# Attention and expert kernel on one core: prologue on VectorE, V projected ahead of q and k, values in four matmuls with a last sum on GpSimd

## What is computed

```python
def bi_wkv(r, k, v, w, u, time_emb):        # forward and backward decayed sums over T
    tf = sigmoid(sum(time_emb, -1))[:, None, None]
    decay = exp(-exp(w))[None, :] * (0.5 + 0.5 * tf[:, :, 0])
    ek = exp(minimum(k, 30.0)); ekv = ek * v
    nf, df = scan(ekv), scan(ek); nb, db = reverse scans
    euk = exp(minimum(u + k, 30.0))
    base = sigmoid(r) * ((nf + nb - ekv + euk * v) / maximum(df + db - ek + euk, 1e-8))
    return base * (0.8 + 0.2 * tf)
def attn(x, W_K, W_Q, W_V, W_O):            # 16 heads of 128, causal
    k, q, v = (einsum('ihd,bpd->biph', W, x) for W in (W_K, W_Q, W_V))
    z = softmax(masked(q k^T) / sqrt(128)) v
    return einsum('df,bqf->bqd', W_O, z_flat)
def ffn(x, gate_w, expert_w, expert_b):     # 8 experts, top 2, softmax of the two gates
    ...
x = x + attn(bi_wkv(x, fside, fside, w, u, cond), ...)
x = x + ffn(bi_wkv(x, fside, fside, w2, u2, cond), ...)
```

## Time and profile before

| | us |
|---|---|
| median of 3 runs | 388.52 (388.48 to 388.64) |
| the profiled execution, its own time | 388.69 |
| its span (first to last instruction) | 386.8 |
| TensorE busy | 357.1 (92%), 2534 matmuls |
| VectorE busy | 315.2 (81%) |
| ScalarE busy | 219.7 (57%) |
| GpSimd busy | 210.1 (54%) |

### The profile page before, as it was taken

One profiled execution on the slowest core, in us unless ns is written; L12 is line 12 of the kernel. 1 busy time (PEld: TensorE's weight loads), 2 busy tenths in 40 slices (PEclk: granted clock), 3 DMA queues, 4 the chain that ended last, 5 costly groups with the idle time before them and its releaser, 6 DMA issues.

```text
span 386.8 us, 7608 instructions
## 1 busy us (share of the span) xinstructions
PE 357.1 (92%) x2534; PEld 332.8 (86%) x2534; DVE 315.2 (81%) x883; ACT 219.7 (57%) x616; POOL 210.1 (54%) x231
## 2 busy tenths in 40 slices
PE   0578888999999999999999999999999998999996
PEld 0467878999999899999999999999999987877885
DVE  3979988897889788988988898889757694676675
ACT  3648567648655766775667576665666463221000
POOL 3677977645553567956865776677554333110000
PEclk9999899999999999999999999999999999999999
DMA  6651050010000000031100004100000000000000
GB/s 219 217 170 50 0 164 2 19 39 1 2 0 2 1 3 2 11 110 47 53 3 2 1 20 146 56 2 1 3 0 2 2 1 3 0 14 14 28 29 27
DMA packets 4598, 14.14 MB, mean 37 GB/s; under 512 B 840, under 2 KB 1872, under 8 KB 3920
## 3 DMA queue, kind: packets, MB, share of 16 engines
q1 hardware_dynamic: 4416, 13.65, 10.6%
q10 hardware_dynamic: 144, 0.00, 0.0%
HBM read 12.60 MB, written 1.05 MB: 35 GB/s over the span
## 4 chain that ended last, share of the span: by engine, by line
PE 81%; DVE 10%; issue 2%; POOL 2%; ACT 2%; DMA 1%; SPq 0%; DVEq 0%; ACTq 0%; POOLq 0%
PE psQK L850 9%; PE psQK L852 9%; PE psQK L851 9%; PE psT L910 5%; PE psZ L850 4%; PE psO L852 4%; PE psO L850 4%; PE psO L851 4%; PE psS L901 4%; PE psS L850 4%; PE psZ L852 4%; PE psZ L851 4%; PE psS L851 4%; PE psS L852 4%; PE psV L850 4%; PE psV L852 3%
## 5 line engine op out<-in xcount | busy, mean ns | idle before, releaser
L472 ACT ACTIVATE prob<-prob,ntop 128x256 f32<-128x256 f32 (+1 forms) x128 | 57.3, 449 | 93.3 <-DVE ntop L690 93.3
L301 POOL TENSOR_SCALAR prob<-prob,rsum 128x128 f32<-128x128 f32 x64 | 38.9, 607 | 104.7 <-DVE rsum L698 104.7
L850 PE MATMUL psQK<-y_hi,w_hi 128*128 128x256 f32 x256 | 73.3, 286 | 1.3 <-DVE y_lo L613 1.1
L852 PE MATMUL psQK<-y_hi,w_lo 128*128 128x256 f32 x256 | 73.0, 285 | 0.0
L851 PE MATMUL psQK<-y_lo,w_hi 128*128 128x256 f32 x256 | 72.9, 285 | 0.0
L302 POOL TENSOR_SCALAR prob<-prob,rsum 128x256 f32<-128x256 f32 x64 | 59.8, 935 | 0.0
L266 POOL TENSOR_TENSOR w_lo<-raw,w_hi 128x512 fp32r<-128x512 f32 x40 | 52.9, 1334 | 6.6 <-ACT w_hi L356 6.4
L850 PEld LDWEIGHTS psQK<-y_hi,w_hi 128*128 128x128 f32 x256 | 49.3, 193 | 2.2 <-DVE y_lo L613 1.3
L852 PEld LDWEIGHTS psQK<-y_hi,w_lo 128*128 128x128 f32 x256 | 49.3, 193 | 0.0
L851 PEld LDWEIGHTS psQK<-y_lo,w_hi 128*128 128x128 f32 x256 | 49.3, 193 | 0.0
L702 DVE TENSOR_TENSOR qk<-psQK,qk 128x512 fp32r<-128x512 f32 x64 | 43.6, 682 | 6.5 <-ACT qk L460 4.8
(11 more groups left out here) (176 smaller groups left out, 1044.3 us busy)
## 6 DMA issues: line engine op xcount, KB each, us to landing
raw<-in_weights SPq DMA_DIRECT2D x5, 1024.0 KB, 6.5
raw<-in_weights SPq DMA_DIRECT2D x10, 512.0 KB, 4.2
out<-fT SPq DMA_DIRECT2D x8, 128.0 KB, 2.0
fT<-in_fT SPq DMA_DIRECT2D x2, 256.0 KB, 6.5
xT<-in_xT SPq DMA_DIRECT2D x2, 256.0 KB, 8.4
fT<-in_fT SPq DMA_DIRECT2D x1, 512.0 KB, 10.2
xT<-in_xT SPq DMA_DIRECT2D x1, 512.0 KB, 10.9
wu<-in_wu ACTq DMA_DIRECT2D x1, 4.0 KB, 1.6
```

What stands on the lines that cost most here:

```text
L301: pool.tensor_scalar(prob[:, k, 0:P], prob[:, k, 0:P], rsum[:, k, 0:1], None, ALU.mult)
L472: ins = act.activation(prob[:, k, lo:hi], prob[:, k, lo:hi], ACT.Exp, scale=-1.0, bias=ntop[:, k, q:q + 1], accum_out=ssum[:, k, q:q + 1])
L850: pe.matmul(out, ah, bh, start=first and k == 0, stop=False)
L852: ins = pe.matmul(out, al, bh, start=False, stop=last and k == n - 1)
```

## The change

1. *values*: the transposed probabilities pT are stored without their zero block, high and low side by side (3 x 128 columns each). Four matmuls take the place of six: v_hi of key block 0 against high and low of both query blocks (512 columns, the whole bank psZ), v_lo against the high part (256), and for key block 1 v_hi and v_lo against high and low of the second query block (2 x 128 columns each). So the low part's products are summed in the second half of psZ. z_high copies both halves (512 columns, z_two), z_low subtracts as before, and a new GpSimd addition, z_last, adds the second half to z_lo; output waits for it. z_last(u - 3) stands at the head of unit u on GpSimd, ahead of its list and of shares(u).
2. *V order*: project_v stands right behind scores(u), V(0, 0) ahead of scores(0). v_high stands behind exps(u), v_low behind reciprocals(u).
3. *Prologue*: SP loads f0 first and waits for it before the next load; temb goes to ScalarE's queue. The three products of GpSimd are gone: f_ekv and f_eukv are made on VectorE in PSUM; ScalarE saves one exp and its double copies of euk. WARM is 5.
4. *Places*: min and exps of a cond stand a unit earlier; refills of V units stand in "M" for groups above 1; shares of units 2 and 3 run on ScalarE; the tile y2 is gone, y2 lives in the cond tiles.
5. *End*: gates_copy(0) stands in unit 62, gates_turn(1) behind the output in unit 63, pT_high(63) ahead of tanh(2), y2_last(3) ahead of gate_last(2), and `late` is shifted by one in three places.

```diff
-DVE_PLACES = {"min": (-2, "E"), "xd": (0, "M"), ...
+DVE_PLACES = {"min": (-3, "E"), "xd": (0, "M"), ...
-ACT_PLACES = {"exps": (-1, "E"), "sxd": (0, "E"), ...
+ACT_PLACES = {"exps": (-2, "E"), "sxd": (0, "E"), ...
+SHARES_ACT = (2, 3)
-WARM = 7
+WARM = 5
-    pT = sb("pT", [P, 2, 2, 4 * P], F32R)
-    z_hi = sb("z_hi", [P, 2, GH, T], F32R)
+    pT = sb("pT", [P, 2, 2, 3 * P], F32R)
+    z_two = sb("z_two", [P, 2, GH, 2, T], F32R)
+    z_hi = z_two[:, :, :, 0]
-    f_ek, f_euk = halves(psQK[0]), halves(psS[0])
+    f_ek, f_ekv, f_euk, f_eukv = (halves(bank) for bank in (psQK[0], psQK[1], psS[0], psT))
 sync:
-        sp.dma_start(temb[:], ap["temb"]).then_inc(in_temb, 16)
         load_f(0, 1, in_f0)
+        sp.wait_ge(in_f0, 16)
         load_qk(0)
 gpsimd:
-        pool.memset(pT[:, :, :, 0:P].bitcast(F32), 0.0).then_inc(consts, 1)
+        def z_last(u):
+            i, h = u // GH, u % GH
+            pool.wait_ge(z_half, u + 1)
+            pool.tensor_tensor(z_lo[:, i % 2, h], z_lo[:, i % 2, h].bitcast(F32), z_two[:, i % 2, h, 1].bitcast(F32),
+                               ALU.add).then_inc(z_ready, 1)
-        pool.tensor_tensor(t0[:, EKV], t0[:, EK], cols(fT, 0), ALU.mult).then_inc(f_pool, 1)
-        pool.tensor_scalar(t0[:, EUK], t0[:, EUK], EXP_LIMIT, None, ALU.min).then_inc(f_pool, 1)
-        pool.tensor_tensor(f_eukv, t0[:, EUK], cols(fT, 0), ALU.mult).then_inc(f_pool, 1)
         for u in range(UNITS):
+            if u >= 3:
+                z_last(u - 3)
             for f, args in work.get(u, ()):
                 f(*args)
-            shares(u)
+            if u not in SHARES_ACT:
+                shares(u)
+        for u in range(UNITS - 3, UNITS):
+            z_last(u)
 scalar:
-            act.activation(z_hi[:, i % 2, h], psZ[:, 0:T], ACT.Copy).then_inc(z_hi_done, 1)
+            act.activation(z_two[:, i % 2, h], halves(psZ), ACT.Copy).then_inc(z_hi_done, 1)
-                at(u, "E", refill, kind, g, part)
+                at(u, "M" if u % GH < TT and g > 1 else "E", refill, kind, g, part)
         for u in range(UNITS):
             exps(u)
+            if h < TT and u:
+                v_high(i, h)
             do(u, "M")
...
+            if u in SHARES_ACT:
+                shares(u)
...
-            if h < TT:
-                v_high(i, h)
 vector:
+        dve.tensor_tensor(f_ekv, f_ek, cols(fT, 0), ALU.mult).then_inc(f_dve, 1)
...
+        dve.scalar_tensor_tensor(f_eukv, f_euk, EXP_LIMIT, cols(fT, 0), ALU.min, ALU.mult).then_inc(f_dve, 1)
...
         for u in range(UNITS):
-            if 1 <= u:
-                i, h = (u - 1) // GH, (u - 1) % GH
-                if h < TT:
-                    v_low(i, h)
             maxima(u)
             do(u, "M")
             reciprocals(u)
+            i, h = u // GH, u % GH
+            if h < TT:
+                v_low(i, h)
 tensor, values(u):
-            three(psZ[:, 0:T],
-                  [(both(v_hi, v_lo, ALL, i % 2, kb, slice(h * DH, (h + 1) * DH)),
-                    (pT[:, k, 0, (1 - kb) * T:(2 - kb) * T], pT[:, k, 1, (1 - kb) * T:(2 - kb) * T]))
-                   for kb in range(TT)]).then_inc(pv_done, 1)
+            heads = slice(h * DH, (h + 1) * DH)
+            second = psZ[:].rearrange("p (a n) -> p a n", a=2)[:, :, P:T]
+            pe.matmul(psZ[:], v_hi[:, i % 2, 0, heads], pT[:, k, :, P:3 * P], start=True, stop=False)
+            pe.matmul(psZ[:, 0:T], v_lo[:, i % 2, 0, heads], pT[:, k, 0, P:3 * P], start=False, stop=False)
+            pe.matmul(second, v_hi[:, i % 2, 1, heads], pT[:, k, :, 0:P], start=False, stop=False)
+            pe.matmul(second, v_lo[:, i % 2, 1, heads], pT[:, k, :, 0:P], start=False, stop=True).then_inc(pv_done, 1)
 tensor, units:
+        project_v(0, 0)
             scores(u)
+            if h < TT and u:
+                project_v(i, h)
...
-            if h < TT:
-                project_v(i, h)
-            elif i:
+            if h >= TT and i:
                 output(i - 1, h - TT)
-        late = {7: [(logits, 3)], 9: [(gates_turn, 2)], 10: [(base, 2)], 11: [(gates_turn, 3)], 12: [(base, 3)]}
+        late = {8: [(logits, 3)], 9: [(gates_turn, 2)], 10: [(base, 2)], 12: [(gates_turn, 3)], 13: [(base, 3)]}
```

More of the change, by code:

```diff
@@ L178, in cols @@
         return t[:, b]
+    y2 = [tiles[:, b % 2, GD + b // 2] for b in range(B)]
     def halves(bank):
         return bank[:].rearrange("p (c n) -> p c n", c=2)
-    f_ek, f_euk = halves(psQK[0]), halves(psS[0])
+    f_ek, f_ekv, f_euk, f_eukv = (halves(bank) for bank in (psQK[0], psQK[1], psS[0], psT))
     f_xd, f_xn = [psV[:, 0:T], psS[1][:, 0:T]], [psZ[:, 0:T], psO[:, 0:T]]
     t0 = tiles[:, 0]
-    f_e1, f_eukv = t0[:, XD], t0[:, XN]
+    f_e1 = t0[:, XD]
     def w_view(t, kind, part):
@@ L310, in y2_low @@
             pool.wait_ge(y2hi_done, b + 1)
[L311 removed]
+            pool.tensor_tensor(cols(y_lo, b), y2[b], cols(y_hi, b).bitcast(F32), ALU.subtract).then_inc(y2lo_done, 1)
         work = {}
@@ L379, in _ @@
         for c in range(CB):
-            act.activation(f_euk[:, c], fT[:, 0, c], ACT.Exp, bias=wu[:, 1, c:c + 1]).then_inc(f_act, 1)
-        for c in range(CB):
-            act.wait_ge(f_dve, 4 + c)
+            act.wait_ge(f_dve, 5 + c)
             scaled(f_xn[c], 0, c, 0).then_inc(f_act, 1)
@@ L474, in exps, with shares @@
             ins.then_inc(exped, 1)
+        def shares(u):
+            k = u % 2
+            act.wait_ge(recipd, u + 1)
+            act.activation(prob[:, k, 0:P], prob[:, k, 0:P], ACT.Copy, scale=rsum[:, k, 0:1])
+            act.activation(prob[:, k, P:3 * P], prob[:, k, P:3 * P], ACT.Copy, scale=rsum[:, k, 1:2]).then_inc(shared, 1)
         def pT_high(u):
@@ L507, in _ @@
         at(62, "E", gate_exp, 1)
-        at(63, "M", gates_copy, 0)
+        at(62, "E", gates_copy, 0)
         at(63, "E", gates_copy, 1)
@@ L522, in _ @@
         qk_high(1)
+        v_high(0, 0)
         cond(1)["exps"]()
         for u in range(UNITS):
+            i, h = u // GH, u % GH
             exps(u)
+            if h < TT and u:
+                v_high(i, h)
             do(u, "M")
@@ L533, in _ @@
             do(u, "E")
-            i, h = u // GH, u % GH
-            if h < TT:
-                v_high(i, h)
         z_high(UNITS - 2)
+        pT_high(UNITS - 1)
         tanh(2)
-        pT_high(UNITS - 1)
         z_high(UNITS - 1)
@@ L834, in _ @@
         add_experts(5)
+        y2_last(3)
         gate_last(2)
-        y2_last(3)
         add_experts(6)
         add_experts(7)
+        add_experts(8)
         gate_first(3)
-        add_experts(8)
+        add_experts(9)
         gate_last(3)
-        for j in range(9, 8 * B):
+        for j in range(10, 8 * B):
             add_experts(j)
@@ L949, in logits @@
                 for c in range(CB):
-                    ins = pe.matmul(bank[:, o:o + E], y2[:, b, c, t * P:(t + 1) * P], gate_w[:, c], start=c == 0, stop=c == CB - 1)
+                    ins = pe.matmul(bank[:, o:o + E], y2[b][:, c, t * P:(t + 1) * P], gate_w[:, c], start=c == 0, stop=c == CB - 1)
             ins.then_inc(logits_done, 1)
@@ L1006, in _ @@
         pe.matmul(ts, ones[:], temb[:], start=True, stop=True).then_inc(tsummed, 1)
-        pe.wait_ge(consts, 3 + E)
-        pe.wait_ge(f_dve, 6)
+        pe.wait_ge(consts, 2 + E)
+        pe.wait_ge(f_dve, 7)
         for n in range(WARM):
             for c in range(CB):
-                pe.matmul(psQK[1][:, c * T:(c + 1) * T], identf[:], fT[:, 0, c], start=True, stop=True)
+                pe.matmul(psQK[0][:, c * T:(c + 1) * T], identf[:], fT[:, 0, c], start=True, stop=True)
         pe.wait_ge(wlo_qk, 2)
-        pe.wait_ge(f_dve, 18)
+        pe.wait_ge(f_dve, 20)
         project_qk_half(0, 0)
@@ L1043, in _ @@
             if u == UNITS - 1:
+                gates_turn(1)
                 base(0)
```

80 lines of the change are left out of this document (37 added, 43 removed).

## The result

The changed kernel takes **386.71 us** (median of 20 runs, 383.48 to 388.60) against 388.52 before (388.30 to 388.69): a ratio of 0.9954, 95% interval 0.9938 to 0.9970. It is faster by 1.8 us, where 16.2 were forecast (372.3), and outside the forecast's range of 368 to 380. The runs of before lie within 0.4 us, those of after spread over 5, longer where the mean granted clock was lower (383.48 at 0.994, 387.7 to 388.6 at 0.978), and the profiled execution is among the long ones (388.28, span 386.5, clock 0.981). So stages are compared between profiles, and kernels by their medians.

The account below looks back on a forecast made before the run. TensorE was taken to bound the kernel from 63.4 us on, VectorE from 27.0 to 63.4. Gains 6.8 + 3.1 - 2.0 + 4.0 + 1.5 + 2.8 = 16.2 gave 372.3 us, range 368 to 380.

Parts of the forecast that it names:

- z_last, priced at nothing: GpSimd's 64 additions, at most 0.67 us each, fit its free time and cost nothing if the cover holds.
- rival (e): Steady units: z_last holds VectorE and pushes GpSimd's products onto scans; 5.1 us a unit, 408 us in all; 6%.
- the half microsecond spare takes it: Steady units: VectorE's spare time per unit absorbs a hold by z_last of at most 0.67 us.
- Values, 6.8: Units 7 to 59: four matmuls for six save 0.1275 us of TensorE a unit, 6.8 us gained.
- rival (c): Values: the new matmul forms cost the old time, so 7.3 us is missing, 379.6 us; 5%.
- V order, 3.1: Values in one unit of eight: TensorE's 0.62 us wait for V's low part goes, five times, 3.1 us gained.
- pT's new waits, -2.0: Units with V: pT's copies have less time before values; 0.15 us a block, 2.0 us lost.
- Rival (a): Units with V: pT becomes late in every block, 0.65 us in each of 14, 379.4 us; 15%.
- Start, 4.0: Before scores(0): f0 lands earlier and additions read PSUM, so q/k's second half starts 4.35 us earlier; 4.0 us gained.
- rival (b): Start: f0 no faster alone, or idle time lowers the clock; 1.5 of 5.5 us stay, 376.3 us; 12%.
- First seven units, 1.5: VectorE-bound first units: a TensorE wait at 60.87 can go and shares move to ScalarE; 1.5 us gained.
- End, 2.8: After 301.5 us: single TensorE waits go through moved pieces, less z_last(63)'s delay and disturbance; 2.8 us gained.

Follow-up runs that it names:

- no_sum: Changed kernel without the 64 GpSimd additions z_last, the second half of the bank copied but never added: 377.64 us.
- undo_values: Changed kernel with values back to six matmuls into half the bank and no GpSimd addition; prologue and V order stay new: 382.75 us.
- vorder_alone: Kernel before with only the new order of V, and the refills and cond pieces moved with it: 387.21 us.
- prologue_alone: Kernel before with only the new prologue and tail, y2 tiles and shares of units 2 and 3 on ScalarE: 384.91 us.

## Why the prediction failed, point by point

Cut at the starts of scores of units 0, 7 and 63, the profiled executions of before, of after and of the kernel without the addition are:

| stretch | before | after | no_sum | gain forecast | gain of after |
|---|---|---|---|---|---|
| to scores(0) | 27.04 | 26.07 | 24.40 | 4.0 | 1.0 |
| to scores(7) | 36.40 | 38.34 | 37.96 | 1.5 | -1.9 |
| to scores(63) | 257.89 | 258.25 | 249.45 | 7.9 | -0.4 |
| to the end | 65.5 | 63.8 | 63.8 | 2.8 | 1.7 |

The addition accounts for 9.1 us of the miss. Without it the kernel (377.64) lands inside the range, still 5.3 above the 372.3; these lie in the start, the first units and the end.

- **z_last, priced at nothing: the step that failed.** The prediction added nothing to the sum for it beyond a share of the 2.0 of new waits. It cost 8.8 us between scores(7) and scores(63) (258.25 for 249.45), and 9.1 by the medians. Of the 8.8, 7.0 had come by scores(55); the last 1.8 lie where the clock stood at half from 318 to 321 us in the changed kernel and not in no_sum. Its own duration was sized well enough (0.75 us for the estimated 0.67), and both effects had been named, in rival (e): that it holds VectorE and that it pushes the other products onto the scans. The error was "the half microsecond spare takes it". VectorE's added busy time is (35.46 - 32.80) / 8 = 0.33 us a unit, below that half microsecond and far below the 0.74 from which (e) was said to decide. But it doesn't come evenly. It comes in units with scans, 1.5 us at once, and the low part of V that TensorE waits for stands right behind: 0.85 us of TensorE in one unit, nothing in the next. A spare that is a mean over eight units was set against a load that falls on a few. Rival (e) had the right mechanism at too high a price, a unit of 5.1 us where 4.5 came in this period (36.04 / 8) and 4.6 on the mean of units 7 to 62, so the result lies between the forecast's range and (e), where no case of mine stood.
- **Values, 6.8: the matmuls as forecast, somewhat less of it in the time.** From 194.73 to the turn at 195.31 the four matmuls take 0.58 us, for 0.59 forecast, so rival (c) is out; a period falls by 1.00 us between undo_values and no_sum, 0.125 a unit. From scores(7) to scores(55), 48 units, it is 4.9 us (216.14 less 211.21) for the 6.1 that 0.1275 a unit gives; the earlier periods gained less. By the medians of these two it is 5.1 us.
- **V order, 3.1: right between the profiles.** From scores(7) to scores(55) vorder_alone takes 216.08 us for 219.22, 3.1 less with pT's new waits included; by the medians it is 1.4. It also laid three pairs of scans beside GpSimd's products, which the forecast had not.
- **pT's new waits, -2.0: in few places, not in every block.** In the periods of no_sum and undo_values shown above TensorE never waits. In no_sum three waits ahead of psZ stand between scores(7) and scores(63), 0.50, 0.54 and 1.36 us. The 7.5 us ahead of psZ in the changed kernel are five waits: 3.0 and 1.3 in the first units, 1.6 near the end and only two of 0.78 in between, in 14 blocks. Rival (a) is out.
- **Start, 4.0: 1.0 came, for two reasons.** f0 landed at 3.95 (3.6 forecast; its lower bound was the time of 128 KB on the way out, and f0 is 256 KB on the way in), but temb, 1 KB, now first in ScalarE's queue, landed at 4.10, and the chain runs from it. The first scan began at 6.04 for 7.58 before, 1.5 us earlier and not 2.6. That temb's own path would be the longer one I had not weighed:

```profile
0.73 3.37 DMA temb<-in_temb
4.23 0.57 PE psO L1029 x2
4.83 0.18 ACT tf L379
5.23 0.19 DVE tf L576
...
12.66 1.11 DVE tout L616
...
14.35 0.65 DVE thalf L621
15.00 0.33 DVE psV L625
15.33 0.33 DVE psS L625
15.66 1.66 DVE tiles L816
```

The chain from there was not "about even" either: two small operations, tout and thalf, take 1.11 and 0.65 us of it while GpSimd refills weights, and the reciprocal began at 15.58 for 16.47. Behind it the additions from PSUM took 0.40 for 1.11 and 1.50, as forecast (1.75). So q and k could start 2.7 earlier. Second, rival (b): TensorE stood idle for 3.6 us ahead of the first projection and then ran it at half clock. The same part in no_sum, where TensorE stood idle there for 2.09 us and the granted clock stayed at 1.00, has scores(0) at 24.40, so 1.7 earlier (0.4 of it is the first projection, 19.83 for 20.25). In the changed kernel, busy times and clock (0.65, 0.50) from 20 us on:

```profile
20.00:22.00 2.00, 1.75 (x9) 1.78 (x10) 1.52 (x5) 1.00 (x3) 0.02 (x1) 0.65 0.51 127
22.00:24.00 2.00, 2.00 (x12) 2.00 (x11) 0.17 (x1) 0.42 (x1) 2.00 (x2) 0.50 0.90 295
```

- **First seven units, 1.5: wrong in sign.** V(0, 1) waited 1.84 us for V's low part, and half clock came back at 31 and at 44.5 us behind idle time. But with the clock at 1.00 these units were not shorter than before either: 36.49 us in undo_values and 36.66 in prologue_alone, for 36.40. The new prologue had nothing to win in this stretch, which VectorE sets.
- **End, 2.8: 1.7.** The waits at 324.34 and 345.86 went. A new one of 0.92 us came at 349.11 (gates_turn, behind the exponent's chain on VectorE), and the one ahead of psZ, whose 0.7 was to go too, grew from 0.72 to 1.63, put down to pT, and half clock followed from 318 to 321 (both ahead of scores(63), so in the table's third row).

The range failed with the same step: 368 to 380 left out the case in which VectorE is the bound in a few units only.

## What to carry to other kernels

Price an operation that is added to GpSimd by what stands behind it in its queue, and look where that will fall on the partner's two-operand work; the instruction's own time is here the smaller part. Weigh it against the slack of the unit in which it falls, not against a mean over a period. And where several parts are changed together, try each alone: here prologue and V order gave 5.8 us, and the third part took 4 of them back.

## What the runs showed of the hardware

- VectorE's scans (both inputs in SBUF) and GpSimd's two-input operations wait for each other. The two scans of the place shown first, one by one:

```profile
216.31 1.08 DVE L590 TENSOR_TENSOR_SCAN tiles<-decay,tiles 128x256 f32<-128x256 f32 x1
...
217.31 1.72 DVE L590 TENSOR_TENSOR_SCAN tiles<-decay,tiles 128x256 f32<-128x256 f32 x1
```

  The addition runs from 216.10 to 216.84 at its usual length. The first scan, begun behind it, ends at 217.39, 0.55 us after it. den's addition, begun at 216.81, ends at 218.49, 1.10 us after that scan, and the second scan ends at 219.03, 0.54 after den's addition. Alone, a scan takes 0.66 and den's addition 1.30. It is the same all over the changed kernel: 32 scans from 30 us on began while a two-input operation of GpSimd ran, they took from 0.68 to 1.78 us, and each ended 0.55 to 0.62 us behind that operation. The Trainium skill ("SBUF — State Buffer", the section on the two sides) calls the shared port pair an exclusive lock, under which the loser fully blocks. For a scan against a two-input operation this trace agrees.
- A one-input operation of GpSimd holds a scan too, but not for its whole length. In the earlier trace rows the scans began 0.60 us and more behind the clamp's start and were not held. In six of the clamp's seven places in the changed kernel a scan was running when it began, and the next scan began 0.38 to 0.44 us behind the clamp's start; that scan took 1.03 us instead of 0.66, ended 0.34 before the clamp did, and the clamp took 1.75 to 1.81 us instead of 1.49:

```profile
176.75 1.75 POOL L286 TENSOR_SCALAR tiles<-tiles 128x512 f32<-128x512 f32 x1
...
177.13 1.03 DVE L590 TENSOR_TENSOR_SCAN tiles<-decay,tiles 128x256 f32<-128x256 f32 x1
```

  So the prediction's argument that a scan beside a tensor_scalar was not held was true of the place where the two met, not of the kind of operation.
- A load of 1 KB issued first in its queue took 3.37 us to land, and 256 KB issued at the same time in another queue landed 0.15 us before it (in the changed kernel).
